# Attention and ternary feed-forward on one core: all instruction orders laid anew, the masks in one load, gelu's average moved from GpSimd to VectorE

## The reference

```python
    x = x + _L0_xattn_ref(_layernorm(x, axis=-1), ctx_2048, mask_BxS2_bk0)
    x = x + _L0_ffn_ref(_layernorm(x, axis=-1), L0_ffn_w1, ..., L0_ffn_b2)

    # attention: scores = einsum(x, ctx) / sqrt(512); masked -> -1e30; softmax; readout = attn @ ctx
    def act_quant(x):
        scale = 127.0 / jnp.clip(jnp.max(jnp.abs(x), axis=-1, keepdims=True), 1e-05)
        q = jnp.clip(jnp.round(x * scale), -128.0, 127.0) / scale
    def weight_quant(w):
        scale = 1.0 / jnp.clip(jnp.mean(jnp.abs(w)), 1e-05)
        q = jnp.clip(jnp.round(w * scale), -1.0, 1.0) / scale
    def bitlinear158(x, w, b):
        return jnp.einsum('bsd,od->bso', act_quant(rms_norm(x)), weight_quant(w)) + b

    h = jax.nn.silu(bitlinear158(x, w1, b1))          # 512 -> 2048
    h = jax.nn.gelu(h, approximate=False)
    h = layer_norm(h, ln_g, ln_b)
    return bitlinear158(h, w2, b2)                    # 2048 -> 512
```

## Time and profile before

| | us |
|---|---|
| median of 3 runs (418.84 to 422.11) | 419.87 |
| the profiled execution | 421.23 |
| its span, first to last instruction | 419.4 |
| busy in the span: PE | 384.0 (92%) |
| ACT | 381.8 (91%) |
| DVE | 365.9 (87%) |
| POOL | 271.8 (65%) |
| the granted clock of PE, mean | 0.983 of full |

### The profile page before, as it was taken

How to read it: one execution, slowest core, us unless ns; L and a number is a source line. 1 busy time by engine, 2 the same in 40 slices (tenths; PEclk the granted TensorE clock), 3 DMA queues, 4 the chain that set the end, 5 groups by cost and what they waited for, 6 DMA issues and landing times.

```text
span 419.4 us, 6830 instructions
## 1 busy us (share of the span) xinstructions
PE 384.0 (92%) x1878; PEld 204.7 (49%) x1878; DVE 365.9 (87%) x571; ACT 381.8 (91%) x517; POOL 271.8 (65%) x373
## 2 busy tenths in 40 slices
PE   3899988789999999999999999999999987899996
PEld 2667353535545544544555454554455532344342
DVE  5278669989998989999999999989998789999992
ACT  1497999999999999999999999999999999999960
POOL 5358488764687838764785569585468855477930
PEclk9999998899999999999999999999999996999999
DMA  7998992556755677669668757694654423083484
GB/s 278 409 312 301 359 342 69 153 162 142 211 147 131 188 193 184 103 189 204 155 169 249 190 166 148 199 222 107 174 135 106 91 63 63 2 200 102 87 214 128
DMA packets 110389, 73.87 MB, mean 176 GB/s; under 512 B 87048, under 2 KB 87056, under 8 KB 109584
## 3 DMA queue, kind: packets, MB, share of 16 engines
q1 hardware_dynamic: 110352, 73.43, 65.1%
HBM read 44.05 MB, written 8.39 MB: 125 GB/s over the span
## 4 chain that ended last, share of the span: by engine, by line
issue 25%; ACT 21%; DVE 19%; PE 17%; POOL 13%; DMA 4%; SPq 1%; DVEq 0%; POOLq 0%; ACTq 0%
ACT junk_v L1212 6%; DVE hid L1981 5%; DVE hid L1972 5%; PE z L624 4%; PE acc L649 4%; ACT hid L1201 3%; ACT hid L1207 3%; POOL hid L1618 3%; PE ba L574 3%; ACT junk_l L1223 2%; POOL rstd L1607 2%; DVE am L1986 2%; POOL xc L1563 2%; DVE st L1900 1%; DMA hid<-in_w2T_dram 1%
## 5 line engine op out<-in xcount | busy, mean ns | idle before, releaser
L624 PE MATMUL z<-w1q,q1T 128*128 128x512 f16 x512 | 124.0, 386 | 3.3 <-ACT hid L1201 3.1
L649 PE MATMUL acc<-w2q,q2T 128*128 128x512 f16 x512 | 117.4, 379 | 0.4 <-DMA q2T<-hid 0.4
L1981 DVE SCALAR_TENSOR_TENSOR hid<-hid,rstd,beta 128x2048 f32<-128x2048 f32 x32 | 76.8, 2402 | 6.2 <-POOL rstd L1607 5.9
L624 PEld LDWEIGHTS z<-w1q,q1T 128*128 128x128 f16 x512 | 49.9, 99 | 65.6 <-ACT hid L1201 9.7
L1972 DVE SCALAR_TENSOR_TENSOR hid<-hid,nmu,gain 128x2048 f32<-128x2048 f32 x32 | 79.3, 2480 | 0.4 <-POOL nmu L1599 0.3
L649 PEld LDWEIGHTS acc<-w2q,q2T 128*128 128x128 f16 x512 | 49.8, 98 | 58.2 <-issue 0.9
L1986 DVE TENSOR_REDUCE am<-hid 128x1 f32<-128x2049 f32 x32 | 72.5, 2269 | 0.1
L1201 ACT ACTIVATE hid<-z,fac 128x1024 f32<-128x1024 f32 x64 | 70.7, 1119 | 1.6 <-PE z L629 1.4
L1223 ACT ACTIVATE junk_l<-hid 128x2050 bf16<-128x2050 f32 x32 | 61.1, 1910 | 4.1 <-DVE hid L1981 4.0
L1618 POOL TENSOR_SCALAR hid<-hid,kq 128x2048 f16<-128x2048 f32 x30 | 60.9, 2031 | 4.6 <-DVE kq L1993 3.1
L1212 ACT ACTIVATE junk_v<-hid,gsum 128x2048 bf16<-128x2048 f32 x32 | 63.7, 1990 | 0.1
(11 more groups left out here) (105 smaller groups left out, 572.2 us busy)
## 6 DMA issues: line engine op xcount, KB each, us to landing
ctxT<-in_ctxT_dram SPq DMA_DIRECT2D x32, 256.0 KB, 3.5
xs<-in_x_dram SPq DMA_DIRECT2D x32, 256.0 KB, 3.9
xT<-in_xT_dram SPq DMA_DIRECT2D x32, 256.0 KB, 3.6
ctx<-in_ctx_dram SPq DMA_DIRECT2D x32, 256.0 KB, 3.4
out_dram<-xs SPq DMA_DIRECT2D x32, 256.0 KB, 3.0
hid<-in_w1T_dram SPq DMA_DIRECT2D x4, 1024.0 KB, 10.2
hid<-in_w2T_dram SPq DMA_DIRECT2D x4, 1024.0 KB, 7.8
gain<-in_g_dram SPq DMA_DIRECT2D x1, 1024.0 KB, 11.1
```

Source lines behind the costliest of these rows:

```text
L624: pe.matmul(z_ps[h][:, c * CH:(c + 1) * CH], q1T[:, t % 4, k, :], w1q[:, k, f0:f0 + CH], start=(k == 0), stop=False)
L649: mm = pe.matmul(a, q2T[:, t % 2, c, :], w2q[:, c, :], start=False, stop=(c == FC - 1))
L1981: dve.scalar_tensor_tensor(out=hh, in0=hh, scalar=rstd[:, t:t + 1], in1=beta[:, :], op0=ALU.mult, op1=ALU.add).then_inc(s_l, 1)
```

## The change

It has these parts:

1. All five lists are laid anew. The loop over tiles 12 to 19 on ACT is written out, and `warm` is called 14 times in place of 20.
2. The masks of all 32 tiles come in one transfer of 32 x 128 bytes in place of 8, and `mask_bias` makes them one tile `maskb` (a row for each tile) at the start, in place of 8 steps of 4 tiles. `scores(t)` picks its row with column t of the identity, stretched over 128 columns, in place of a matrix of ones.
3. `gelu_mean(t)` runs on DVE in place of POOL.
4. Waits: `silu(t)` of tiles 4 to 7 waits for the rounding of the one block of w2 whose row it overwrites, in place of all four blocks rounded and clamped; `turn_factors` waits for the previous copy of its own bank only; the order of some waits within a step changes.

```diff
             def scores(t):
                 wait(pe, s_centred, t)
                 if t == 0:
-                    pe.wait_ge(s_const, 1)
-                pe.wait_ge(s_maskb, t // G + 1)
-                pe.matmul(score_ps, ones_b[:, :], maskb[:, t // G % 2, t % G, :], start=True, stop=False)
+                    pe.wait_ge(s_identb, 1)
+                    pe.wait_ge(s_maskb, 1)
+                pe.matmul(score_ps, ident_b[:, t:t + 1].to_broadcast((P, P)), maskb[:, :], start=True, stop=False)
...
-                wait(pe, s_o, b - 1)
-                wait(pe, s_brow, s)
+                wait(pe, s_brow, s if b <= 0 else s - 1)
                 pe.wait_ge(s_bsp[3], s + 1)
...
             def silu(t, h):
-                act.wait_ge(s_z[h], t + 1)
                 act.wait_ge(s_zs, t + 1)
                 if 4 <= t < 8:
-                    for c in range(4):
-                        act.wait_ge(s_w2q[c], STEPS)
+                    act.wait_ge(s_w2q[t - 4], 1)
                 if t >= HR:
                     act.wait_ge(s_q2T[t % 2], landed(t - HR, 2))
+                act.wait_ge(s_z[h], t + 1)
...
-            def mask_bias(g):
-                if g == 0:
-                    pool.wait_ge(s_const, 1)
-                pool.wait_ge(s_mask[g % 2], landed(g, 2))
-                wait(pool, s_score, G * (g - 1))
-                pool.tensor_scalar(maskb[0:1, g % 2, :, :], mask[:, g % 2, :, :], MASKED, -MASKED,
-                                   ALU.mult, ALU.add).then_inc(s_maskb, 1)
+            def mask_bias():
+                pool.wait_ge(s_const, 1)
+                pool.wait_ge(s_mask, 16)
+                pool.tensor_scalar(maskb[0:NT, :], mask[:, :], MASKED, -MASKED, ALU.mult, ALU.add).then_inc(s_maskb, 1)
...
-            def gelu_mean(t):
-                pool.wait_ge(s_gelu, t + 1)
-                pool.tensor_scalar(nmu[:, t:t + 1], gsum[:, t:t + 1], -1.0 / FF, 0.0,
-                                   ALU.mult, ALU.add).then_inc(s_nmu, 1)
...
+            def gelu_mean(t):
+                dve.wait_ge(s_gelu, t + 1)
+                dve.tensor_scalar(nmu[:, t:t + 1], gsum[:, t:t + 1], -1.0 / FF, None, ALU.mult).then_inc(s_nmu, 1)
```

More of the change, by code:

```diff
@@ L975, in _ @@
+            readout(25)
             second_product(14, 0)
@@ L1305, in _ @@
[L1305 to L1311 removed]
+            gelu(4)
+            silu(5, 0)
+            silu(5, 1)
+            variance(4)
+            silu(6, 0)
+            square_x1(8)
+            mean_term(14)
+            silu(6, 1)
+            gelu(5)
+            copy_probT(10)
+            square_x1(9)
+            mean_term(15)
+            square_l(2)
@@ new lines, in _ @@
+            mean_term(19)
+            square_x1(14)
+            square_x1(15)
+            silu(12, 0)
+            copy_probT(16)
+            variance(10)
+            silu(12, 1)
+            square_l(8)
+            square_l(9)
+            gelu(11)
+            gelu(12)
+            exp_scores(17)
+            mean_term(20)
+            exp_scores(18)
+            mean_term(21)
+            exp_scores(19)
+            copy_probT(17)
+            variance(11)
+            square_x1(16)
+            copy_probT(18)
@@ new lines, in _ @@
+            exp_scores(20)
+            silu(13, 0)
+            silu(13, 1)
+            variance(12)
+            silu(14, 0)
+            copy_probT(19)
+            square_l(10)
+            silu(14, 1)
+            square_x1(17)
+            silu(15, 0)
+            square_l(11)
+            silu(15, 1)
+            gelu(13)
+            mean_term(22)
+            copy_probT(20)
+            variance(13)
+            mean_term(23)
+            gelu(14)
+            gelu(15)
+            exp_scores(21)
@@ new lines, in _ @@
+            variance(14)
+            variance(15)
+            copy_probT(21)
+            square_x1(18)
+            square_x1(19)
+            exp_scores(22)
+            silu(16, 0)
+            silu(16, 1)
+            square_l(12)
+            square_l(13)
+            mean_term(24)
+            silu(17, 0)
+            copy_probT(22)
+            mean_term(25)
+            silu(17, 1)
+            gelu(16)
+            gelu(17)
+            exp_scores(23)
+            exp_scores(24)
+            square_l(14)
@@ L1448, in _ @@
-            gelu(24)
+            variance(22)
+            variance(23)
+            copy_probT(28)
+            silu(24, 0)
+            silu(24, 1)
+            square_l(20)
+            silu(25, 0)
+            square_l(21)
+            silu(25, 1)
+            gelu(24)
+            gelu(25)
+            exp_scores(29)
+            square_x1(28)
+            exp_scores(30)
+            copy_probT(29)
+            variance(24)
+            variance(25)
+            exp_scores(31)
+            silu(26, 0)
@@ new lines, in _ @@
+            normed(0)
+            gained(1)
+            x1_absmax(4)
+            copy_factors(3)
+            x1_absmax(5)
+            x_stats(11)
+            normed(1)
+            q1_scale(4, 2)
+            add_readout(6)
+            clamp_w2(0)
+            norm_absmax(0)
+            z_scale(4, 2)
+            softmax(9)
+            add_readout(7)
+            invert_factors(4, 2)
+            gelu_mean(2)
+            x_stats(12)
+            x_stats(13)
+            x_stats(14)
+            softmax(10)
@@ new lines, in _ @@
+            prob_sum(11)
+            gelu_mean(6)
+            gained(5)
+            q2_scale(2, 2)
+            normed(5)
+            add_readout(11)
+            copy_factors(8)
+            softmax(15)
+            copy_factors(9)
+            prob_sum(12)
+            x_stats(16)
+            norm_absmax(4)
+            prob_sum(13)
+            norm_absmax(5)
+            x_stats(17)
+            add_readout(12)
+            x1_absmax(10)
+            out_scale(4, 2)
+            x1_absmax(11)
```

2044 lines of the change are left out of this document (926 added, 1118 removed).

## The result

| | before | after |
|---|---|---|
| median of all runs | 419.78 us (418.84 to 422.11, 4 runs) | 425.94 us (425.02 to 429.21, 4 runs) |
| profiled execution, its span | 421.23 us, 419.4 us | 429.21 us, 427.4 us |

The ratio is 1.0158, with an interval of 1.0121 to 1.0195: **slower by 1.6%**. The forecast was 419.3 us, no change. The profiled execution of after is the slowest of its four; the spans of the other three are 423.2 to 424.6 us. So some 3 of the 8 us between the two traces belong to this one execution, and one question is what makes it so.

A forecast was written before the change was run, and what follows sets the result against it. ACT was taken to set the middle's pace, transfers the front. Terms -0.4 + 0 + 0.4 - 0.3 - 0.3 = -0.6 took the span from 419.4 to 418.8 us; adding 0.47 gave 419.3, range 411.5 to 426.

The forecast's parts named there:

- w2's last block: Front: it lands near 54.5 us, ACT reaches its sum at 55 to 56, so later landing costs 0 to 1 us.
- w2's last block is late: Front: issued behind load_ctx(5), which needs readout(3); a 5 us slip gives 424.3; chance 0.09, with other misfits.
- ACT's idle time up to 60 us: Front: ACT idles 18.7 us against 19.14, so -0.4 us, with bounds of -2.4 and +3.
- silu(0,0) at 38 (36 to 40): Front: ACT's first silu of tile 0 starts at 38 us, bounds 36 and 40, against 40.59 before.
- Table loads 0: ACT: front 3 more, middle 3 fewer, cancelling at 3.9 us; tail 2 fewer; booked 0, bounds -2.6 and +1.
- Tail: -0.3 - 0.3 + 0.4 forecast: POOL's relief -0.3 us, split_factors(34) earlier on POOL and PE -0.3, the last four gelu averages on DVE +0.4.
- price with a drain: ACT: the skill page's 2.66 us per table switch would give 415.3 us; given no more than 0.01.
- gelu's average, +0.4: DVE: 32 one-column operations, 4.9 us at most; 0 in the middle's idle time, +0.4 us in the tail.
- POOL's relief: DVE's long multiply-adds: 14 of POOL's 272 us go, worth -0.3 us, bounds 0 and -0.9.
- Masks, 0: PE: the masks' product keeps its size with another stationary operand; 0, at worst 32 x 0.1 us.
- Middle stalls, 0: ACT from 80 to 400 us: idle time stays 4.1 us, so 0, with bounds of -3 and +6.
- The likeliest case: Whole kernel: small terms cancel and nothing matters; range of its own 415.7 to 424 us, chance 0.40.

The follow-up runs named there:

- experiment 15: Changed kernel with load_ctx(2) ahead of w2's first block, plus matmuls on unused data in TensorE's waits ahead of turn_factors(30) and (34); 423.96 us, 1.0086.
- experiment 3: Kernel before with its own lists, plus masks in one load, gelu_mean on DVE ahead of each gained, and silu's new waits; 420.88 us, 1.0035.
- experiment 13: Experiment 9 with TensorE's list too as before from behind first_product(28,1), its warm calls included; 430.72 us, 1.0254.
- 9: Experiment 1 with ACT's, DVE's, POOL's and SP's old list ends from behind variance(29), norm_absmax(29), gelu_rstd(28) and store(22); 423.84 us, 1.0097.
- experiment 4: Changed kernel with gelu(30) moved back on ACT to directly behind silu(30, 1), its variance behind square_l(27); 429.74 us, 1.0258.
- experiment 6: Changed kernel with old list ends: ACT's from gelu(28), DVE's from gained(29), POOL's from centre_x1(31), SP's from store(20); 425.05 us, 1.0152.
- experiment 1: Changed kernel with load_ctx(2) ahead of the first block of w2 instead of behind its first two blocks; 424.88 us, 1.0133.
- experiment 17: Experiment 15 with POOL's gelu_rstd(31, 1) one place earlier, ahead of round_q2(29) and norm_kappa(30, 1); 424.12 us, 1.0097.

## Why the prediction was wrong

By its own steps:

- **w2's last block, "costs 0 to 1 us": the step that failed first.** The arithmetic asked when 2.4 MB more would have landed, 54.5 us. The block landed at 61.7. ACT reached its sum at 59.8, not at 55 to 56, and waited 1.92 us for it; it had lost the rest before, in waits for w2's second block (2.12 us), the exponential's bias (1.13) and the product of tile 1 (0.80). It wasn't bytes that held it but its place behind load_ctx(5), and that behind readout(3), which follows readout(2), which waited for ctx(2). The rival "w2's last block is late" named this queue and its end, but not this trigger: it looked at ACT's copy, which was done at 47.2, while readout(3) came at 50.28 behind the slow scores(4) and (5); the load of ctx(2), put behind two blocks of 1 MB, was passed over in the sum. It had been issued at 18.27 us and now went at 30.58. ACT's idle time up to 60 us: -0.4 forecast, +3.6 in the profiled execution, and +5.4 up to 80 us. The low clock alone put the block's issue back by 3.5 us. In the median the place of either transfer is worth about 1 us.
- **silu(0,0) at 38 (36 to 40):** 36.71. Right, and worth nothing, because the wait for w2 and readout(2) comes behind it.
- **Table loads 0:** the 45 loads are as counted, and 2.4 us of work went from ACT. The bound of +1 for gelu(30) was too small: gelu(30) slipped by 12.8 us and gained(30) by 9.8, where gelu(31) slipped by 4.2. DVE then has six passes of 2.3 us from gained(30) on with nothing to fill, and normed(31) follows gelu(31) by 10.6 us, not 7.2. Tail: -0.3 - 0.3 + 0.4 forecast, +1.7 from gelu(29) on in the trace. One slip stands in the prediction's working: its price with a drain, 415.3, took off the middle's three switches and left out the front's three more, which by the same price cancel them. Every load in this trace is followed by the next step 0.02 us later at most, so that price plays no part.
- **The clock:** no term at all. It held back w2's last block by 3.5 us in the profiled execution, and in the tail holding it gave 1.5 us in the trace (experiment 15: 0.47% in the ratio, with intervals that overlap). In the changed kernel's own trace it also lies on the chain that ended last: a second product of 16 matmuls takes 5.14 us at 406.60, and the next 3.45. The new list has fewer warming matmuls at the end, as the diff shows.
- **gelu's average, +0.4:** 1.1 us measured, 0.27% [0.09, 0.45]. The mechanism was as put, and the forecast stands at the interval's lower end; the likely reason, that the middle isn't free for it, wasn't tested. As to POOL's relief, the long steps of DVE are shorter in the trace (2459 and 2358 ns for 2480 and 2402), by 2 us in all; but the first takes 2404 in experiment 15, whose DVE list is the same, and with the old order and POOL's steps gone (experiment 3) the second takes 2391. The longest of them begin inside one of POOL's long steps (gained at 230.31, 3.18 us, inside a rounding from 229.38 to 231.35), and the roundings weren't taken away. So how much of it is the relief and how much the order isn't shown.
- **Masks, 0:** right.
- **Middle stalls, 0:** +1.3 us. Inside the bounds, on the slow side.

The account in the ratios, in per cent: average on DVE 0.27, ctx(2)'s place 0.25, clock at the end 0.47, which leaves 0.6, or 2.5 us, of the 1.58. Of that rest only the place is seen. gelu(29) to the end is as before in experiment 15, so it lies ahead of gelu(29); ACT idles there 1.5 us more from 80 to 400 us (5.65 for 4.13), in waits such as 0.98 us for the product, up to 166.77, which recur with 0.97 or 0.98 us in every execution of this order. Which of the moved lines makes them wasn't isolated, nor whether the new waits by bank do. The two middle shares are differences of overlapping intervals, so the split is an estimate.

The likeliest case was chosen because the terms were small; but they were small because each was sized alone, against waits that the same change moved.

## What to carry to other kernels

When a load moves behind larger ones, follow its first reader and then everything that waits in that reader's queue; the bytes say when the last transfer can land, the queue says when it is issued. Price each new wait of TensorE twice, as time and as the work behind it at half the clock, and look whether the change takes warming matmuls out. Lists written out for several engines are one plan: swapping the end of four or five of them, which should have undone the tail, cost up to 7 us more than it gave (experiment 13 against 9), and only the trace between two fixed marks showed what it had given.

## What the hardware showed that wasn't expected

**The same lists, different fronts.** With the changed kernel's front gelu(2) starts at 82.17, 79.57 (experiment 4) and 76.30 us (experiment 6), a spread of 5.9; with the old one at 70.23 to 72.06 in four executions. From there on, executions of this order agree to 0.1 us over 290 us: the changed kernel's lag behind experiment 1, which differs from it by one load's place, is 4.57 us at gelu(2) and 4.65 at gelu(29). ctx(2) comes 2.1 us sooner in experiment 6 (PE idles 2.69 us, not 4.10), and there the high clock stays. In experiment 4, behind a wait of 3.86 us, readout(2) still runs at the high clock (1.10 us) and the scores from 43.67 us on at the low one (2.02 us). The Trainium skill, page "TensorE: Matmul & The Clock Gate", section "What's actually happening", says that the same kernel sees the change of clock at other points from run to run; these traces agree, and show it amplified by the queues behind.

**POOL's short steps stretch to DVE's long ones.** On POOL the step on 128x4 elements takes 0.20 us at 392.84, beside a reduction on DVE, and 2.21 at 400.83, ending as normed(30) (2.35 us from 400.62) ends. The one on 128x1 takes 0.19 us at 55.88, 0.53 at 399.35, near the end of gained(30) (397.48 to 399.82), and 1.98 at 406.41, inside gained(31) (406.00 to 408.3). The Trainium skill, page "GPSIMD Engine Reference", section "Key points", has the two engines share their SBUF interfaces, with contention for DVE instructions that read two tensors there; the rows agree, and put a size on it: the short step lasts until the long one is over. It goes the other way as well: in experiment 4 gained(30) starts at 398.76 inside a rounding of POOL's (1.97 us from 398.06) and takes 3.41 us. In experiment 1, where the two short steps stood in the chain that ended last, they held 4.2 us of it; experiment 17 shows that this isn't to be won by moving them, since DVE's own steps last as long.
